# A decoder block's last layer: row columns taken from transposed tiles, products in three float32r terms, the expert choice moved behind a shift

## The chip, the core and the metric

The kernel runs on one core of a Trainium2 chip. TensorE does matrix products and transposes into PSUM, VectorE and ScalarE work on SBUF and PSUM, GpSimd on SBUF alone; SyncE and the others issue DMAs. The metric is the device time of one execution in microseconds; the median of several runs counts.

## The reference

Two transformer layers on x of 2 batches x 1024 rows x 256 columns. Each layer is a cross attention over 64 context rows with 16 heads, and a feed-forward part. The change touches only the second layer's end:

```python
def _layernorm(x, axis=-1, eps=1e-05):
    m = jnp.mean(x, axis=axis, keepdims=True)
    v = jnp.var(x, axis=axis, keepdims=True)
    return (x - m) / jnp.sqrt(v + eps)
...
    def _L1_ffn_ref(x, Wr, A, Bw):
        ...
        def _gates(cls_tok, Wr):
            logits = cls_tok @ Wr.T
            top_vals, top_idx = jax.lax.top_k(logits, K)
            neg_inf = jnp.full_like(logits, -jnp.inf)
            rows = jnp.arange(logits.shape[0])[:, None]
            masked = neg_inf.at[rows, top_idx].set(top_vals)
            return jax.nn.softmax(masked, axis=-1)
        gates = _gates(x[:, 0, :], Wr)
        mid = jnp.einsum('blh,erh->belr', x, A)
        expert_out = jnp.einsum('belr,ehr->belh', mid, Bw)
        weighted = jnp.einsum('be,belh->blh', gates, expert_out)
        return x + weighted
...
    x = x + _L1_xattn_ref(_layernorm(x, axis=-1), ctx_1024, ctx_1024, L1_xattn_Wq, L1_xattn_bq, L1_xattn_Wk, L1_xattn_bk, L1_xattn_Wv, L1_xattn_bv, L1_xattn_Wo, L1_xattn_bo)
    x = x + _L1_ffn_ref(_layernorm(x, axis=-1), L1_ffn_Wr, L1_ffn_A, L1_ffn_Bw)
```

The experts of a batch are chosen by its first row alone (K = 2 of E = 8, R = 64). So for each batch the kernel makes one 256x256 matrix, the weighed sum of the two experts' products, and multiplies every normalised row by it.

## The kernel before

The rows lie in 16 tiles of 128; two tiles make a unit, so there are NU = 8 units, even ones of batch 0, odd ones of batch 1. Each engine has one hand-written program, and semaphores tie them; what stands first in an engine's program runs first, and a wait holds all behind it.

The second attention runs unit by unit. Within step u, TensorE does scores(u,0), transposes of unit u-1's second half, the transposes of the next unit, project_o(u-2), values(u-1), scores(u,1), the query projection of the next unit (project_q), and the transposes of unit u's first half. VectorE does shift(u,0) and shift(u,1) (maximum, L507, and subtraction, L510) and between them the weighing of unit u-1 (weigh: L516, L519, L522, which makes oT). ScalarE does exponentials, copies out of PSUM and the logarithm in front of the weighing (L453, L455). GpSimd adds biases (L606) and subtracts the projected rows from x (residual, L613), and makes the reciprocal deviations of the norms (L115, L117).

The last layer's work is threaded into this loop by four tables (tensor_work, scalar_work, vector_work, gpsimd_work). Key 2u is a slot inside step u ahead of its second half, 2u+1 is its end, 16 lies behind the loop, "end" behind project_o(7). The steps of unit u of this last layer are: stats3 (VectorE), rstd3 (GpSimd), normalise3 (ScalarE), turn3 (four transposes on TensorE into one PSUM bank), copy3 (ScalarE), product3 (TensorE), add_norm (GpSimd adds the norm to x), add3 (VectorE adds the product), store (SyncE).

The choice of experts goes beside it: row_stats, row_rstd and row_norm normalise the two first rows alone, on one partition (L1617 to L1632); row_columns turns them into columns with eight tiny products (L1641); spread_columns copies each column to 128 (L1649); row_logits multiplies by the router weights (L1658); choose finds the two best experts (L1665 to L1675) with top_two; gates computes the weights; pick_factors gathers the two factors with indirect DMAs (L1702); weigh_second_factor scales one of them; batch_matrix makes the matrix (L1717) and keep_matrix copies it. product3 is in float32.

## Time and profile before

| what | value |
|---|---|
| time, median of 3 runs | 493.1 us (491.43 to 493.35) |
| the profiled execution's own time | 497.36 us |
| its span, from first to last instruction | 495.5 us |
| mean granted TensorE clock | 0.992 |
| busy: TensorE, VectorE, ScalarE, GpSimd | 95%, 58%, 40%, 48% of the span |

The times in the rows count from the span's start. A float32 product is two records of TensorE. The second attention begins at about 376 us; the last products end at 492.2 us, and the last store lands by 495.5 us.

### The profile page before, as it was taken

The page shows a single profiled execution, that of the slowest core. Times are in us where ns is not written, and L with a number is a line of the kernel's source. Part 1 is how long each engine was busy: PE and PEld are TensorE (multiplying, and loading weights), DVE is VectorE, ACT ScalarE, POOL GpSimd, SP SyncE. Part 2 cuts the span into 40 slices and gives each one's busy share as a digit, 9 for nine tenths or more (in the row PEclk, how much of TensorE's full clock was granted, in tenths as well). Part 3 has the DMA queues.
Part 4 walks back from the last instruction along what each step waited for, and adds up shares of the span by engine and source line. Part 5 has one row for each costly group of instructions (what it writes and reads, how often), then busy time and mean ns, then how long its engine had stood idle before and what let it go on. Part 6 is the DMA issues. An engine that isn't in the chain of part 4 may idle for free.

```text
span 495.5 us, 9491 instructions
## 1 busy us (share of the span) xinstructions
PE 468.4 (95%) x3132; PEld 385.0 (78%) x3132; DVE 286.6 (58%) x657; ACT 199.5 (40%) x447; POOL 236.0 (48%) x315
## 2 busy tenths in 40 slices
PE   7899999998999997998999999999997999899797
PEld 6677776686777786677999999999977676677576
DVE  5779985643461122325454545545457689998862
ACT  3455775557610021002323333232332456665641
POOL 6313344144337574219985543233232665753462
PEclk9999999999999999998999999999999899999999
DMA  8999300020003122999413332223117300000114
GB/s 280 392 404 351 41 12 1 1 85 2 0 1 111 69 103 84 340 309 331 70 48 102 108 87 70 82 65 86 34 42 238 104 2 1 1 3 0 31 34 150
DMA packets 48031, 52.98 MB, mean 107 GB/s; under 512 B 15313, under 2 KB 42258, under 8 KB 47730
## 3 DMA queue, kind: packets, MB, share of 16 engines
q1 hardware_dynamic: 34578, 23.02, 16.8%
q0 software_dynamic: 7616, 20.19, 12.3%
q10 hardware_dynamic: 5792, 9.18, 6.2%
q8 instruction: 28, 0.46, 0.4%
q14 instruction: 17, 0.14, 0.1%
HBM read 35.25 MB, written 17.12 MB: 106 GB/s over the span
## 4 chain that ended last, share of the span: by engine, by line
PE 75%; DVE 12%; ACT 4%; DMA 3%; issue 2%; another core or an unknown queue 1%; POOL 1%; ACTq 1%; SPq 0%; POOLq 0%; DVEq 0%
PE banks L1285 9%; PE banks L1232 9%; PE banks L1336 6%; PE banks L346 5%; PE banks L360 5%; PE banks L1337 5%; PE banks L1340 5%; PE banks L324 5%; PE banks L313 3%; PE banks L1358 3%; PE banks L1766 3%; PE banks L1362 3%; PE banks L1359 3%; PE banks L1348 3%; DVE mx L507 2%
## 5 line engine op out<-in xcount | busy, mean ns | idle before, releaser
L115 POOL TENSOR_TENSOR rstd<-var,mhalf 128x2 f32<-128x2 f32 x30 | 20.9, 696 | 86.1 <-DVE var L108 86.1
L1336 PE MATMUL banks<-w_hi,xgT_hi 128*128 x156 | 55.5, 356 | 2.8 <-ACT xgT_hi L966 2.3
L1162 ACT ACTIVATE hg<-banks 128x352 f32<-128x352 f32 x39 | 18.2, 466 | 98.6 <-PE banks L1340 89.0
L1509 DVE TENSOR_TENSOR hgT_lo<-banks,hgT_hi 128x256 fp32r<-128x256 f32 x78 | 24.1, 350 | 58.1 <-ACT hgT_hi L1169 56.7
L507 DVE TENSOR_REDUCE mx<-banks 128x16 f32<-128x1024 f32 x32 | 39.1, 1220 | 23.9 <-PE banks L324 23.7
L1337 PE MATMUL banks<-wd,xgT_hi 128*128 x156 | 51.0, 328 | 0.0
L1285 PE MATMUL banks<-sdn,big 128*128 128x256 f32 x192 | 47.5, 393 | 0.0
L1285 PEld LDWEIGHTS banks<-sdn,big 128*128 128x128 f32 x192 | 34.1, 189 | 12.6 <-issue 9.0
L1063 POOL DMA_INDIRECT expert_rows_in<-xn,slot x32 | 31.4, 982 | 20.7 <-issue 7.7
L324 PE MATMUL banks<-kvb,qT 64*128 64x256 f32 x256 | 36.7, 406 | 3.3 <-DVE ps L510 2.1
L1340 PE MATMUL banks<-w_hi,xgT_lo 128*128 x156 | 37.9, 325 | 0.0
L125 ACT ACTIVATE xn<-x,shift,rstd 128x256 f32<-128x256 f32 x60 | 32.9, 604 | 9.7 <-POOL shift L117 9.5
L1131 ACT ACTIVATE pw<-banks 128x512 f32<-128x512 f32 (+1 forms) x24 | 14.2, 593 | 53.0 <-issue 29.0
L1232 PE MATMUL banks<-xn2T_hi,sgu_hi 128*128 128x512 f32 x80 | 31.9, 399 | 2.9 <-DVE big L1475 2.9
L1336 PEld LDWEIGHTS banks<-w_hi,xgT_hi 128*128 128x128 f32 x156 | 29.9, 192 | 5.0 <-issue 4.5
L324 PEld LDWEIGHTS banks<-kvb,qT 64*128 64x128 f32 x256 | 22.5, 187 | 13.0 <-issue 9.1
L1094 POOL DMA_INDIRECT choices_out<-yy,dest x18 | 18.1, 1003 | 28.5 <-DVE yy L1502 21.1
L1232 PE MATMUL banks<-xn2T_lo,sgu_hi 128*128 128x512 f32 x80 | 31.2, 391 | 0.0
L1232 PE MATMUL banks<-xn2T_hi,sgu_lo 128*128 128x512 f32 x80 | 31.2, 390 | 0.0
L1358 PE MATMUL banks<-wd,hgT_hi 128*128 (+1 forms) x117 | 29.8, 284 | 0.7 <-ACT hgT_hi L1169 0.7
L1337 PEld LDWEIGHTS banks<-wd,xgT_hi 128*128 128x128 f32 x156 | 30.0, 192 | 0.2
L1359 PE MATMUL banks<-wd,hgT_hi 128*128 (+1 forms) x117 | 29.8, 283 | 0.0
(249 smaller groups left out, 1137.0 us busy)
## 6 DMA issues: line engine op xcount, KB each, us to landing
w_hi<-in_egu POOLq DMA_DIRECT2D x2, 2816.0 KB, 21.3
expert_rows_in<-zeros SPq DMA_DIRECT2D x1, 5304.0 KB, 40.3
xn<-expert_rows_in SPq DMA_DIRECT2D x39, 128.0 KB
y_all<-choices_out SPq DMA_DIRECT2D x16, 256.0 KB, 4.9
wd<-in_egu ACTq DMA_DIRECT2D x8, 352.0 KB, 9.7
wd<-in_egu ACTq DMA_DIRECT2D x4, 704.0 KB, 13.8
out_x<-x SPq DMA_DIRECT2D x8, 256.0 KB, 2.1
x<-in_x SPq DMA_DIRECT2D x2, 768.0 KB, 7.6
```

Of the source, the lines that this page charges most:

```text
L125: nc.scalar.activation(out[:, t, :], x[:, first + t, :], ACT.Identity, bias=m["shift"][:, b, t:t + 1], scale=m["rstd"][:, b, t:t + 1]).the ...
L324: last = nc.tensor.matmul(psS[:, r * 512 + hf * 256:r * 512 + hf * 256 + 256], qT[rows, u % 2, hf, t * P:(t + 1) * P], kb[batch_of(u)][row ...
L346: last = nc.tensor.matmul(psO[32 * j:32 * j + 32, k, w, :], lhs, pT[u % 2][:, 4 * k + j, :], start=True, stop=True, tile_position=(0, 32 * j))
L507: nc.vector.tensor_reduce(mx, heads(psS), AX.X, ALU.max).then_inc(max_done.sem, 1)
L1063: pool.indirect_dma_start(xg_dram[:, :], bass.IndirectOffsetOnAxis(ap=slot[:, j, t:t + 1], axis=0), xn2w[:, t, :], None, bounds_check=SLOT ...
L1232: last = nc.tensor.matmul(psum[bank][:, :], m[:, k, w * 6 * P + j * P:w * 6 * P + (j + 1) * P], v[g][:, k, :], start=(a == 0), stop=(a == ...
L1285: last = nc.tensor.matmul(psum[4 + c][:, t * D:(t + 1) * D], hT[0:SR[j], (g + 1) % 2, j, (2 * c + t) * P:(2 * c + t + 1) * P], sdn[0:SR[j] ...
L1336: nc.tensor.matmul(to, xgT_hi[:, c, k, :], hi, start=(k == 0), stop=False)
L1337: nc.tensor.matmul(to, xgT_hi[:, c, k, :], lo, start=False, stop=False)
L1340: last = nc.tensor.matmul(to, xgT_lo[:, c, k, :], w_hi[:, k, ds(e * (2 * I) + w * I, I)], start=False, stop=(k == KD - 1))
L1358: nc.tensor.matmul(psum[6][:, 0:D], h, d(k, 0), start=(k == 0), stop=False)
L1359: nc.tensor.matmul(psum[6][:, 0:D], h, d(k, 1), start=False, stop=False)
```

## The change

The two first rows are no longer normalised apart: the first column of the transposed tiles of units 0 and 1 is the row in question, so spread_columns copies from there (kept, an SBUF copy of the transposed tiles of units 0 to 3), and does it on GpSimd. row_stats, row_rstd, row_norm and row_columns are gone. product3 is split: each operand becomes a high part in float32r and the rest, and three products (high by high, high by low, low by high) take the place of one in float32. High parts of units 0 to 3 are made by ScalarE from kept (high_part), their rests by GpSimd (low_part); for units 4 to 7 the copy out of PSUM is the high part, and VectorE takes the rest (split3); VectorE also splits the matrices (split_matrix). The copy of the logits (take_logits) is split from choose, which moves one slot on. Unit 2 is multiplied before unit 1, the last unit has a PSUM bank for each tile and is added and stored tile by tile.

```diff
         def spread_columns():
-            nc.vector.wait_ge(f_rowT, 1)
-            for b in range(B):
-                for k in range(KD):
-                    v.tensor_copy(xcol[:, b, k, :], PSW[:, b * KD + k:b * KD + k + 1].to_broadcast([P, P])).then_inc(f_col, 1)
...
+            nc.gpsimd.wait_ge(f_xT, B)
...
+                    nc.gpsimd.tensor_copy(xcol[:, b, k, :], kept[:, b, k, 0:1].to_broadcast([P, P])).then_inc(f_col, 1)
...
+        def take_logits():
+            nc.vector.wait_ge(f_lg, 1)
+            v.tensor_copy(gt["p"][:, :, :], PSW[:, 64:64 + B * E].rearrange("p (b e) -> p b e", b=B)).then_inc(f_g, 1)
+
         def choose():
             nonlocal links
-            nc.vector.wait_ge(f_lg, 1)
-            v.tensor_copy(gt["p"][:, :, :], PSW[:, 64:64 + B * E].rearrange("p (b e) -> p b e", b=B)).then_inc(f_g, 1)
             nc.vector.wait_ge(f_g, 1)
...
+        def split_matrix(b):
+            nc.vector.wait_ge(f_wb, b + 1)
+            v.tensor_tensor(wb_lo[:, b, :, :], MATRIX_IN[b].rearrange("p (k n) -> p k n", k=KD),
+                            wb_hi[:, b, :, :].bitcast(F32), ALU.subtract).then_inc(f_wL, 1)
...
         def add_norm(u):
 
             wait(nc.gpsimd, ln3.xn_ready, UT * u + UT)
-            nc.gpsimd.wait_ge(f_row, 1 + B)
...
+            wait(nc.tensor, f_xL, u - KEPT)
...
+            to = kept[:, u, :, :] if u < KEPT else xT3_hi[:, u, :, :]
+            nc.scalar.activation(to, PSX.rearrange("p (k n) -> p k n", k=KD), ACT.Copy).then_inc(f_xT, 1)
+
+        def high_part(u):
+
+            nc.scalar.wait_ge(f_xT, u + 1)
+            nc.scalar.activation(xT3_hi[:, u, :, :], kept[:, u, :, :], ACT.Copy).then_inc(f_hi, 1)
+
+        def low_part(u):
+
+            nc.gpsimd.wait_ge(f_hi, u + 1)
+            nc.gpsimd.tensor_tensor(xT3_lo[:, u, :, :], kept[:, u, :, :], xT3_hi[:, u, :, :].bitcast(F32),
+                                    ALU.subtract).then_inc(f_lo, 1)
+
+        def split3(u):
+
+            nc.vector.wait_ge(f_xT, u + 1)
+            v.tensor_tensor(xT3_lo[:, u, :, :], PSX.rearrange("p (k n) -> p k n", k=KD), xT3_hi[:, u, :, :].bitcast(F32),
+                            ALU.subtract).then_inc(f_xL, 1)
 
         def product3(u):
-            nc.tensor.wait_ge(f_xT, u + 1)
-            nc.tensor.wait_ge(f_wb, min(u + 1, B))
+            nc.tensor.wait_ge(f_wL, u % 2 + 1)
+            if u < KEPT:
+                nc.tensor.wait_ge(f_lo, u + 1)
+            else:
+                nc.tensor.wait_ge(f_xL, u - KEPT + 1)
+                nc.tensor.wait_ge(f_added, ORDER.index(u - 4) + 1)
             if u < 2:
                 wait(nc.tensor, events1["exp_done"], 4 * NU)
-            wait(nc.tensor, f_added, u - 3)
+            terms = [(x, w, k) for k in range(KD) for x, w in ((xT3_hi, wb_hi), (xT3_hi, wb_lo), (xT3_lo, wb_hi))]
             for t in range(UT):
-                for k in range(KD):
-                    last = nc.tensor.matmul(MADE_IN[u][:, t * D:(t + 1) * D], xT3[:, u, k, t * P:(t + 1) * P],
-                                            wb[:, u % 2, k, :], start=(k == 0), stop=(k == KD - 1))
-            last.then_inc(f_y, 1)
+                to = LAST_IN[t][:, 0:D] if u == NU - 1 else MADE_IN[u][:, t * D:(t + 1) * D]
+                for m, (x, w, k) in enumerate(terms):
+                    last = nc.tensor.matmul(to, x[:, u, k, t * P:(t + 1) * P], w[:, u % 2, k, :],
+                                            start=(m == 0), stop=(m == len(terms) - 1))
...
+        def add_last():
+
+            nc.vector.wait_ge(f_summed, NU)
+            for t in range(UT):
+                nc.vector.wait_ge(f_y, NU + t)
+                row = unit_rows(NU - 1)[:, t, :]
+                v.tensor_tensor(row, LAST_IN[t][:, 0:D], row, ALU.add).then_inc(f_added, 1)
...
-        gpsimd_work = {7: lambda: (rstd3(0), first_rows()), 8: row_rstd, 9: lambda: rstd3(1), 11: lambda: (rstd3(2), add_norm(0)),
...
+        gpsimd_work = {7: lambda: (rstd3(0), first_rows()), 9: lambda: rstd3(1),
```

On VectorE, in step 7, the copy of the logits and the start of the choice (gc_ and gt_ are its small tiles) followed the weighing of unit 5 directly; shift(7,0) (mx and ps) came behind all of the choice:

```order
L519 SCALAR_TENSOR_TENSOR ninv<-err,inv 128x512
L522 TENSOR_TENSOR oT<-banks,ninv 128x512
L1665 COPY gt_p<-banks 128x16
L656 TENSOR_REDUCE gc_top<-gt_p 128x2
L657 TENSOR_TENSOR gt_key<-gt_p,gc_top 128x16
```

Now at the same place:

```order
L522 TENSOR_TENSOR oT<-banks,ninv 128x512
L1635 COPY gt_p<-banks 128x16
L507 TENSOR_REDUCE mx<-banks 128x16
L510 TENSOR_TENSOR ps<-banks,mx 128x1024
L656 TENSOR_REDUCE gc_top<-gt_p 128x2
```

The shift of unit 7's first half now stands ahead of the choice, and the choice between the two shifts. Further up on VectorE, stats3(4) has moved from behind the choice to ahead of shift(6,1).

GpSimd's program from step 5 to the gathers, before (L613 is the residual, L115 and L117 the deviations, L1741 add_norm):

```order
L613 TENSOR_TENSOR x<-x,o_rows 128x512
L115 TENSOR_TENSOR rstd<-var,mhalf 128x2
L117 TENSOR_TENSOR shift<-nmean,rstd 128x2
L1741 TENSOR_TENSOR x<-x,xn 128x512
L606 TENSOR_TENSOR x<-x,bo_all 128x256 x2
L613 TENSOR_TENSOR x<-x,o_rows 128x512
```

and now:

```order
L613 TENSOR_TENSOR x<-x,o_rows 128x512
L115 TENSOR_TENSOR rstd<-var,mhalf 128x2
L117 TENSOR_TENSOR shift<-nmean,rstd 128x2
L1620 COPY xcol<-kept 128x128 x4
L1718 TENSOR_TENSOR x<-x,xn 128x512
L1745 TENSOR_TENSOR xT_lo<-kept,xT_hi 128x512
L606 TENSOR_TENSOR x<-x,bo_all 128x256 x2
L613 TENSOR_TENSOR x<-x,o_rows 128x512
```

Four copies and a subtraction stand ahead of residual(4), the last row. Further on, rstd3(4) moves ahead of the residual in front of the gathers, and the gathers follow that residual at once; three more subtractions come in around them.

On TensorE around project_o(7) (L360), before (L1717 is batch_matrix, L1766 product3, L1750 turn3, L346 values(7)):

```order
L346 MATMUL banks<-pT_1,head_ones 32x256 x4
L1717 MATMUL banks<-fbg,fa 128x256 x4
L1766 MATMUL banks<-wb,xT 128x256 x4
L360 MATMUL banks<-wo,oT 128x256 x4
L1750 MATMUL banks<-ident,xn 128x128 x4
L1766 MATMUL banks<-wb,xT 128x256 x8
```

and the start of what stands there now:

```order
L1690 MATMUL banks<-fbg,fa 128x256 x2
L346 MATMUL banks<-pT_1,kvb 32x256 x4
L346 MATMUL banks<-pT_1,head_ones 32x256 x4
L346 MATMUL banks<-pT_1,kvb 32x256 x4
L346 MATMUL banks<-pT_1,head_ones 32x256 x4
L1690 MATMUL banks<-fbg,fa 128x256 x2
L1767 MATMUL banks<-wb_hi,xT_hi 128x256
L1767 MATMUL banks<-wb_lo,xT_hi 128x256
L1767 MATMUL banks<-wb_hi,xT_lo 128x256
```

Half of batch_matrix moved ahead of values(7). The three rows of L1767 repeat: two units of twelve, with turn3(5) between them, now stand ahead of project_o(7), and six units and two transposes behind it. On ScalarE, normalise3(5) and keep_matrix(0) now stand ahead of the last logarithm.

## Rows read from the trace of the kernel before

**Rows 1.** The page: clock in tenths over 40 slices; shares of the chain by engine.

```profile
PEclk9999999999999999998999999999999899999999
PE 75%; DVE 12%; ACT 4%; DMA 3%; issue 2%; another core or an unknown queue 1%; POOL 1%; ACTq 1%; SPq 0%; POOLq 0%; DVEq 0%
```

**Rows 2.** Chain of waits in order of time: start us, us, engine, tile, line, count.

```profile
427.24 1.16 DVE gc_nmean L1620
428.58 0.67 DVE stats L101 x2
...
438.54 0.98 PE banks L1641 x8
...
446.02 0.89 DVE xcol L1649 x4
```

**Rows 3.** Timeline, TensorE's idle times in brackets: start us, us, engine, line, tiles.

```profile
432.35 1.13 PE L324 MATMUL banks<-kvb,qT 64*128 64x256 f32 x8 [1.20 <-DVE ps L510]
...
447.04 1.97 PE L360 MATMUL banks<-wo,oT 128*128 128x256 f32 x8 [0.41 <-DVE xcol L1649]
```

**Rows 4.** The chain of waits further on.

```profile
460.43 1.23 DVE mx L507
...
464.22 1.24 DVE mx L507
...
468.81 1.99 PE banks L360 x8
...
492.20 0.69 DVE x L1775
```

**Rows 5.** Timeline: two GpSimd instructions and what VectorE did beside each.

```profile
409.92 1.29 POOL L613 TENSOR_TENSOR x<-x,o_rows 128x512 f32<-128x512 f32 x1
409.95 1.80 DVE L519 SCALAR_TENSOR_TENSOR ninv<-err,inv 128x512 f32<-128x512 f32 x1
...
467.31 1.02 POOL L1702 DMA_INDIRECT fb<-in_bw,picked  x1 [0.30 <-issue]
467.33 0.70 DVE L519 SCALAR_TENSOR_TENSOR ninv<-err,inv 128x512 f32<-128x512 f32 x1
```

**Rows 6.** Timeline: the choice's first and last instruction, residual, first gather, its use.

```profile
457.62 0.17 DVE L656 TENSOR_REDUCE gc_top<-gt_p 128x2 f32<-128x16 f32 x1
...
460.35 0.17 DVE L1675 CAST picked<-gc_row 128x2 int32<-128x2 f32 x1
...
460.98 1.28 POOL L613 TENSOR_TENSOR x<-x,o_rows 128x512 f32<-128x512 f32 x1 [7.55 <-ACT o_rows L460]
...
465.86 1.15 POOL L1702 DMA_INDIRECT fa<-in_a,picked  x1 [0.62 <-issue]
...
470.47 0.51 ACT L1710 ACTIVATE fbg<-fb,gcol 128x256 f32<-128x256 f32 x1 [1.94 <-DMA fb<-in_bw,picked]
```

**Rows 7.** Groups by line and shape: busy us, mean ns of one, idle before.

```profile
L204 POOL COPY ctx<-ctxT 128x128 f32<-128x128 f32 x4 | 1.4, 389 | 0.0
...
L1017 POOL TENSOR_TENSOR xn2T_lo<-turned,xn2T_hi 128x512 fp32r<-128x512 f32 x2 | 2.5, 1268 | 0.0
...
L1105 ACT ACTIVATE xn2T_hi<-turned 128x512 fp32r<-128x512 f32 x2 | 1.3, 634 | 0.1
```

**Rows 8.** Timeline of TensorE in the experts' down projection (float32r, 256 columns moving).

```profile
301.80 0.28 PE L1358 MATMUL banks<-wd,hgT_hi 128*128 x1
301.92 0.28 PE L1359 MATMUL banks<-wd,hgT_hi 128*128 x1
```

**Rows 9.** Timeline of the end: last logarithm, project_o(7), then transposes and float32 products.

```profile
473.25 0.58 ACT L453 ACTIVATE inv<-banks 128x512 f32<-128x512 f32 x1
...
476.87 1.89 PE L360 MATMUL banks<-wo,oT 128*128 128x256 f32 x8
...
478.60 0.60 PE L1750 MATMUL banks<-ident,xn 128*128 128x128 f32 x4
...
479.04 3.62 PE L1766 MATMUL banks<-wb,xT 128*128 128x256 f32 x16
...
482.49 0.60 PE L1750 MATMUL banks<-ident,xn 128*128 128x128 f32 x4
```

More of the change, by code:

```diff
@@ L1601, in xattn_ffn_kernel @@
         MADE_IN = [psum[(u + 2) % 4] for u in range(NU)]
+        LAST_IN = [psum[(NU + 1) % 4], psum[5]]
+        ORDER = [0, 2, 1, *range(3, NU)]
         def link(ins):
@@ L1804, in load_ffn1 @@
             sp.dma_start(wr[:, :, :], split(wr_in)).then_inc(ffn1_in, 16)
-        tensor_work = {"keys and values": lambda: keep_warm(nc, psum[0], mem["ident"], 26), 9: lambda: turn3(0), 10: row_columns, 11: lambda: turn3(1), 12: row_logits,
-                       13: lambda: turn3(2), 15: lambda: turn3(3), "last output but one": lambda: turn3(4),
-                       16: lambda: (batch_matrix(0), batch_matrix(1), product3(0)),
-                       "end": lambda: (turn3(5), product3(1), product3(2), turn3(6), product3(3), product3(4),
-                                       turn3(7), product3(5), product3(6), product3(7)),
-                       "x6": lambda: nc.tensor.wait_ge(f_xT, 1), "x7": lambda: nc.tensor.wait_ge(f_xT, 2),
-                       "o4": lambda: nc.tensor.wait_ge(f_col, B * KD), "o5": lambda: nc.tensor.wait_ge(f_g, 1)}
@@ L1820, in xattn_ffn_kernel @@
-        vector_work = {6: lambda: stats3(0), 8: lambda: (row_stats(), stats3(1)), 9: lambda: (row_norm(), second_half_rows()), 10: lambda: stats3(2),
-                       11: spread_columns, 12: lambda: stats3(3), 13: choose, 14: lambda: stats3(4), 15: gates,
-                       "last output but one": lambda: stats3(5), 16: lambda: stats3(6),
-                       "end": lambda: (stats3(7), *(add3(u) for u in range(NU)))}
-        gpsimd_work = {7: lambda: (rstd3(0), first_rows()), 8: row_rstd, 9: lambda: rstd3(1), 11: lambda: (rstd3(2), add_norm(0)),
-                       13: lambda: (rstd3(3), add_norm(1)), 15: lambda: (rstd3(4), pick_factors(0), pick_factors(1), add_norm(2)),
-                       16: lambda: (rstd3(5), add_norm(3), rstd3(6), add_norm(4), rstd3(7),
-                                    add_norm(5), add_norm(6), add_norm(7))}
+        tensor_work = {"keys and values": lambda: keep_warm(nc, psum[0], mem["ident"], 26), 9: lambda: turn3(0), 11: lambda: turn3(1), 12: row_logits,
+                       13: lambda: turn3(2), 14: lambda: turn3(3), 15: lambda: turn3(4),
+                       "last output but one": lambda: batch_matrix(0),
+                       16: lambda: (batch_matrix(1), product3(0), turn3(5), product3(2)),
+                       "end": lambda: (turn3(6), product3(1), product3(3), product3(4), turn3(7), product3(5), product3(6),
+                                       product3(7)),
+                       "x6": lambda: nc.tensor.wait_ge(f_xT, 1), "x7": lambda: nc.tensor.wait_ge(f_xT, 2),
+                       "o5": lambda: nc.tensor.wait_ge(f_g, 1)}
@@ new lines, in xattn_ffn_kernel @@
+        vector_work = {6: lambda: stats3(0), 8: lambda: stats3(1), 9: second_half_rows,
+                       10: lambda: stats3(2), 12: lambda: (stats3(3), stats3(4)), 13: take_logits, 14: choose,
+                       15: lambda: (gates(), split3(4), stats3(5)), "last output but one": lambda: (stats3(6), split_matrix(0)),
+                       16: lambda: (split_matrix(1), split3(5), add3(0)),
+                       "end": lambda: (stats3(7), add3(2), add3(1), split3(6), add3(3), add3(4), split3(7), add3(5), add3(6),
+                                       add_last())}
@@ new lines, in xattn_ffn_kernel @@
+        gpsimd_work = {7: lambda: (rstd3(0), first_rows()), 9: lambda: rstd3(1),
+                       11: lambda: (rstd3(2), spread_columns(), add_norm(0), low_part(0)),
+                       13: lambda: (rstd3(3), rstd3(4), add_norm(1), low_part(1), low_part(2)),
+                       15: lambda: (pick_factors(0), pick_factors(1), rstd3(5), add_norm(2)),
+                       16: lambda: (low_part(3), rstd3(6), *(add_norm(u) for u in range(3, 6)), rstd3(7), add_norm(6), add_norm(7))}
```

71 lines of the change are left out of this document (26 added, 45 removed).

## The prediction

> **What bounds the kernel now.** I read the page first, then the chain of waits in order of time, then the timeline of the last 70 us. The page says that TensorE carries 75% of the chain and VectorE 12%, and that TensorE is granted its full clock nearly throughout, the tenths near 1.0 being its 2.4 GHz level [rows 1]. The edits all lie after 425 us of a 495.5 us span, so only that stretch needs pricing. The reader is to see two regimes in it. Up to about 472 us the chain changes hands between VectorE and TensorE: the lone-row statistics stand on it at 427.24, the products that turn the row into a column at 438.54, the spreading at 446.02 [rows 2], and the first score shift of the last unit starts at 460.43, directly behind the expert choice [rows 4, 6]. From 476.87 on it is TensorE alone, with project_o(7), transposes and products to the last add at 492.20 [rows 4, 9]. The two need different working: in the first a removed step gives only what the next late engine leaves; in the second every matmul saved counts whole.
>
> All times below are on the clock of the profiled execution, and are worked as a lead over it. That execution took 497.36 us (span 495.5), the median of the runs is 493.1. I take the gain off the median; a ratio of 0.991 between the two changes a few us by nothing.
>
> **The change in its tail, TensorE alone.** A product in float32 of 128x256 is two records; two units of four products each and one transpose group run from 478.60 to 482.49, of which the transposes take 0.44 (478.60 to 479.04), so a unit costs (3.89 - 0.44)/2 = 1.73 us [rows 9]. The changed unit has 12 float32r products. The nearest row is the expert down projection: float32r, 128x128 weights reloaded for each, 256 columns moving, 0.12 us from one to the next [rows 8]. 12 x 0.1175 = 1.41 us. From the start of project_o(7), before: 1.73 for itself, 3 x 0.44 of transposes, 7 units x 1.73 = 15.2 us. After: only 6 units and 2 transpose groups remain, since product 2 and turn3(5) now stand ahead of project_o(7): 1.75 + 0.9 + 8.5 = 11.1 us. Gain **4.1**, if no wait opens. The one near to opening is turn3(7): residual, statistics, rstd and normalisation of unit 7 take some 4.6 us behind project_o(7), and TensorE has 0.44 + 3 x 1.41 = 4.7 us of work there; I count nothing and keep 0.5 for the range. The last add in halves of 128x256, each stored at once, takes about half of the 0.69 us [rows 4] off the end: gain **0.3**.
>
> **The row's columns.** Leaving out the row statistics on VectorE (427.24 is one of six instructions) lets statistics and shift of unit 4 start that much sooner; what TensorE gets is its own idle time there, 1.2 us before 432.35 [rows 2, 3]. The eight records at 438.54 go: 0.98 us [rows 2]. Against it, ScalarE makes a high part of each kept tile, 0.63 us in the like operation [rows 7], ahead of the normalisation of unit 6, which TensorE's transposes now reach early: loss 0.4. TensorE's wait for the spreading before project_o(4) was 0.41 [rows 3]: gain. Lead by then 2.2 us. Spreading moves to GpSimd: four copies of 128x128 at 0.39 [rows 7] = 1.6 us, followed in the same queue by add_norm(0), low_part(0), the bias add and residual(4), four instructions at about 1.3 us (1.27 for the like subtraction, [rows 7]). GpSimd can start at about 442.9 (the second transposed tile), so residual(4) ends near 449.8. stats3(4) is moved ahead of VectorE's shift (6,1) and waits for exactly that residual; with 1.24 us of its own (428.58 to the next instruction) it ends at 451.1, where the shift's scores are ready at 450.8. Behind it queue the shift and all of TensorE's unit 7. Loss 0.3: lead **1.9 us**. Bounds: copies between nearly 0 and 0.7 each put it at 2.2 and 0.9.
>
> **The choice.** Before, VectorE chose for 2.9 us (457.62 to 460.5, some 14 small instructions [rows 6]) and only then shifted the first half of unit 7. Now only the copy out of PSUM stays ahead and the choice follows that shift. Its place is then between the two shifts, 456.1 + 2.5 = 458.6 to 461.5, where the scores for the second shift are ready at 461.3 anyway: that alone would bring the second shift from 464.22 to 461.5, a lead of 2.7. But now there is GpSimd work beside it. Where a GpSimd add ran beside VectorE's scalar_tensor_tensor with two SBUF operands, it took 1.80 us (409.95, the add at 409.92); beside a gather issue it took 0.70 (467.33) [rows 5]. It looks held until GpSimd's instruction ends. So residual(5), due at 459.4, holds the choice for 0 to 1.2 us. I take it whole: second shift at 462.6, lead **1.6 us**, and 1.4 at project_o(6) (467.4 against 468.81 [rows 4]). The Trainium skill, GPSIMD Engine Reference, section 8 (Key points), states the cause: GpSimd shares its SBUF interfaces with VectorE and contends with VectorE instructions that have two SBUF inputs. By that rule the sum below stands; without it, it would be rival A's.
>
> **The gathers.** They start right behind the choice, no longer behind rstd3(4): at 462.8 against 465.86. The first pair was used 4.6 us after the first issue (470.47 [rows 6]), so it lands at 467.4, before gates() has the weights at 468.0. Thus the gathers' latency, 1.94 us of ScalarE idling, leaves the path. batch_matrix(0) (0.87) now stands before values(7), in place of a transpose (0.44): lead 1.0 at its end.
>
> **The last weighing.** Before, the logarithm started at 473.25 and project_o(7) at 476.87 [rows 9]. Now ScalarE's queue has normalise3(5), which waits for rstd3(5), and keep_matrix(0) ahead of it: 0.5 us lost. VectorE's two-operand step of that weighing now meets add_norm(3) on GpSimd, which is busy without a pause there: up to 1.3, I take 1.0. So project_o(7) starts at about 477.3: lead **-0.4**. If the step isn't held, TensorE still has product 0, turn3(5) and product 2 to do until 476.8, and the lead is about 0.
>
> **Sum.** -0.4 + 4.1 + 0.3 = 4.0 us, 493.1 - 4.0 = **489.1 us**. A measurement of this kernel can tell about 0.5% (2.5 us) from no change.
>
> **Rivals.**
> A, the holds don't bite. If the residual doesn't hold the choice, all behind it comes 1.1 us sooner, and project_o(7) leads by +0.7, or by +1.1 if the weighing isn't held either: gain 5.1 to 5.5, 487.6 to 488.0 us. For it: VectorE's instructions of the choice are short and may get in first.
> B, GpSimd becomes the bound. It takes eight instructions more (four copies, four subtractions, 1.6 + 5.1 us), in a queue through which residual, rstd and gathers pass. Each us that it is late before stats3(4) or rstd3(7) comes off whole; with 1 to 2.5 us lost, the gain is 1.5 to 3: 490.1 to 491.6 us. For it: the 0.3 us by which stats3(4) is late already. Against: GpSimd idled 7.55 us before the residual at 460.98, between units [rows 6].
> C, slower: the pace of the three-term products. It is one mechanism: if a float32r product with changing weights goes at the float32 record's 0.217 us (3.45/16 [rows 9]), not 0.12, a unit costs 2.6 us. Then project_o(7) starts at 479.2 (2.3 late), 6 units behind it cost 15.6 in place of 12.1 with 7, and the end comes 5.0 later: 498.1 us. It decides from 0.165 us a product (24 of them ahead of project_o(7), 72 behind). The down projection's rows speak against it; for it, only that its operands come from other tiles.
> D, it doesn't do what it says: the chain hangs on something untouched. Then about 493. Against it: the tail's products are the chain [rows 4, 9].
>
> **How the numbers follow.** Forecast (3.2 to 5 us gained) 0.50; A 0.22; B 0.19; C 0.04; D 0.05. Over 2.5 us faster: 0.50 + 0.22 + half of B and a little = 0.83; same 0.12; slower 0.05. The range, 486.8 to 491.4, takes A with 0.8 us for the runs' own spread and most of B, and leaves out C and D.
>
> **What would show it.** Right: 12 products of a unit in about 1.41 us; scores (5,0) without idle time; the second shift of unit 7 at 461.5 to 462.6; the first gather right behind the picked rows; 11 to 11.5 us from project_o(7) to the end of the products. Wrong: a product spacing over 0.13; TensorE idle before turn3(7); VectorE idle before stats3(4) for residual(4) by more than 0.5 us; the choice taking over 4.2 us.

## The result and the profile after

The changed kernel takes **486.95 us** (median of 4 runs, 486.51 to 488.73) beside 493.23 us before (4 runs, 491.43 to 494.80): the ratio is 0.9877, with a 95% interval of 0.9842 to 0.9912, so 4.3 to 7.8 us are gained. 489.1 us was forecast. The profiled execution took 488.73 us, with a span of 487.0; before, 497.36 and 495.5.

| us | before | after |
|---|---|---|
| median time | 493.23 | 486.95 |
| span of the profiled execution | 495.5 | 487.0 |
| start of scores(4,1) | 426.44 | 422.87 |
| from there to the end of the span | 69.06 | 64.13 |

The two spans differ by 8.5 us, more than the times, and the last two rows say why. The first place at which both programs do the same work right ahead of the edits is TensorE's scores for the second half of unit 4. It comes 3.57 us sooner after the change, though no edit stands in TensorE's way up to there. The chain of waits of before shows where this is from; its rows are start, duration and what was running:

```profile
178.40 3.11 PE banks L1232 x12
...
181.59 0.69 DVE big L1475
182.28 6.31 another core or an unknown queue
...
189.51 5.73 PE banks L1232 x24
...
196.60 3.41 PE banks L1285 x14
```

The third row is VectorE's wait for something that the profile does not name; TensorE stood idle for 2.95 us of it. The same products in the chain of the changed kernel:

```profile
178.27 13.60 PE banks L1232 x60
...
193.23 6.83 PE banks L1285 x28
```

So something arrived late in that execution of before. The first products of L1285 start at 196.60 there and at 193.23 here, 3.37 us apart. So 3.4 of the 3.6 us belong to one execution. The traces of this study reach scores(4,1) between 420.3 and 426.4 us, though up to there the kernels differ only in a few small instructions (the clamps named below and the first row's statistics). All comparisons of traces below therefore count from scores(4,1). What the edits give by that clock is 69.06 - 64.13 = **4.93 us**, within the interval of the times.

The page of the changed kernel, the chain's shares by engine:

```profile
PE 77%; DVE 7%; ACT 6%; DMA 4%; issue 3%; POOL 1%; ACTq 1%; SPq 0%; POOLq 0%
```

TensorE carries a little more of the chain than before and VectorE less [rows 1]. The chain from the choice to the last add, the counterpart of [rows 2] and [rows 4]:

```profile
456.02 1.24 DVE gt_key L657
458.59 0.59 issue
459.42 0.39 POOL fa L1675
...
463.52 2.94 DMA fb<-in_bw,picked
466.54 0.37 ACT fbg L1683
466.96 1.08 ACT xn L125 x2
468.03 0.49 ACT wb_hi L1696
468.54 0.70 DVE wb_lo L1701
469.29 1.69 PE banks L1767 x12
470.98 0.44 PE banks L1728 x4
471.42 1.43 PE banks L1767 x12
472.85 1.96 PE banks L360 x8
474.81 0.44 PE banks L1728 x4
475.24 4.32 PE banks L1767 x36
479.56 0.44 PE banks L1728 x4
480.00 4.32 PE banks L1767 x36
484.34 0.42 DVE x L1785
```

The last six rows are the tail: from project_o(7) at 472.85 there is no waiting row up to the last add. 36 products of L1767 take 4.32 us, that is 0.12 each and 1.44 for a unit, where a unit had cost 1.73 [rows 9]. Above them stands what the forecast had not put on the path: the landing of the second unit's factors (2.94), and behind it a row of small steps on ScalarE and VectorE that ends at the first product.

VectorE's choice, in its timeline (start, duration, line, operation), and GpSimd's residual beside it:

```profile
454.58 0.16 DVE L656 TENSOR_REDUCE gc_top<-gt_p 128x2 f32<-128x16 f32 x1
454.77 0.17 DVE L657 TENSOR_TENSOR gt_key<-gt_p,gc_top 128x16 f32<-128x16 f32 x1
...
456.02 1.23 DVE L657 TENSOR_TENSOR gt_key<-gt_rest,gc_top 128x16 f32<-128x16 f32 x1
...
458.36 0.17 DVE L1648 CAST picked<-gc_row 128x2 int32<-128x2 f32 x1
458.45 1.22 DVE L507 TENSOR_REDUCE mx<-banks 128x16 f32<-128x1024 f32 x1
```

```profile
455.94 1.27 POOL L613 TENSOR_TENSOR x<-x,o_rows 128x512 f32<-128x512 f32 x1 [2.12 <-ACT o_rows L460]
459.42 1.16 POOL L1675 DMA_INDIRECT fa<-in_a,picked  x1 [2.20 <-DVE picked L1648]
```

The operation of L657 takes 0.17 us at 454.77 and 1.23 at 456.02, beside the residual, and ends 0.04 us after it. This is the hold of [rows 5] again, now on a tile of 128x16. The whole choice takes 3.95 us (454.58 to 458.53), 2.90 before. The first gather starts 0.9 us behind the picked rows.

The stages, each counted in us from the start of scores(4,1), where "shift" is VectorE's maximum (L507) of a half unit, and the leads of after over before next to those that were forecast:

| | shift(6,1) | shift(7,1) | project_o(6) | project_o(7) | end of last add | end |
|---|---|---|---|---|---|---|
| before | 26.53 | 37.78 | 42.37 | 50.43 | 66.45 | 69.06 |
| after | 24.71 | 35.58 | 40.16 | 49.94 | 61.89 | 64.13 |
| lead | 1.82 | 2.20 | 2.21 | 0.49 | 4.56 | 4.93 |
| forecast | 1.9 | 1.6 | 1.4 | -0.4 | | 4.0 |

### The profile page after: what moved, and what is told of

Its sections match the earlier page's. It is cut to its first block, busy times and chain, and to the rows that moved or that the text cites. A ratio compares the mean times of both kernels' runs of the same rounds, so it can differ in the third digit from the quotient of the medians.

```text
span 487.0 us, 9539 instructions
## 1 busy us (share of the span) xinstructions
PE 465.0 (95%) x3156; PEld 383.3 (79%) x3156; DVE 289.7 (59%) x652; ACT 201.2 (41%) x451; POOL 240.8 (49%) x321
## 4 chain that ended last, share of the span: by engine, by line
PE 77%; DVE 7%; ACT 6%; DMA 4%; issue 3%; POOL 1%; ACTq 1%; SPq 0%; POOLq 0%
PE banks L1232 10%; PE banks L1285 10%; PE banks L1336 6%; PE banks L346 5%; PE banks L1337 5%; PE banks L360 5%; PE banks L1340 5%; PE banks L324 5%; PE banks L313 5%; PE banks L1358 3%; PE banks L1362 3%; PE banks L1359 3%; PE banks L1348 3%; PE banks L1767 2%; ACT xn L125 2%
## 5 line engine op out<-in xcount | busy, mean ns | idle before, releaser
L115 POOL TENSOR_TENSOR rstd<-var,mhalf 128x2 f32<-128x2 f32 x30 | 20.8, 695 | 82.6 <-DVE var L108 82.6
L507 DVE TENSOR_REDUCE mx<-banks 128x16 f32<-128x1024 f32 x32 | 39.1, 1221 | 22.5 <-PE banks L324 22.4
L1285 PE MATMUL banks<-sdn,big 128*128 128x256 f32 x192 | 47.5, 393 | 0.0
L1285 PEld LDWEIGHTS banks<-sdn,big 128*128 128x128 f32 x192 | 34.1, 189 | 12.6 <-issue 9.0
```

Of the source, the lines that this page charges most:

```text
L507: nc.vector.tensor_reduce(mx, heads(psS), AX.X, ALU.max).then_inc(max_done.sem, 1)
L1285: last = nc.tensor.matmul(psum[4 + c][:, t * D:(t + 1) * D], hT[0:SR[j], (g + 1) % 2, j, (2 * c + t) * P:(2 * c + t + 1) * P], sdn[0:SR[j] ...
```

## The experiments

Each kernel is the changed one with the edit shown, unless it says before. In all of them the expert numbers that TensorE's registers load are clamped to zero from below, which lets line numbers rise by 3 or 4. Nothing of what is computed is left out in any. Numbers are from the profiled execution, counted from scores(4,1), unless a ratio to the kernel before is given.

**The yardstick.** The changed kernel with only the clamp.

> The changed kernel itself, with one addition that all my kernels carry: the expert numbers that TensorE's program loads are clamped at zero in a second register before they are waited against (40 small register operations, all before the second attention). It is the yardstick for the others. Both theories expect 0.5 us or less beside the changed kernel, so 5 to 7 us under the kernel before, and in its profile the same stretch from the second attention's first product to the last add as in the changed kernel's (some 108.5 us).

487.32 us (6 runs, 486.75 to 489.15), ratio 0.9898 [0.9868, 0.9929]. The stages repeat those of the table within 0.02 us (end 64.13). Two executions of one kernel agree that closely behind scores(4,1), so a few tenths of a us can be read from one trace, as long as the clock stays up (below).

The medians tell less. The same work was timed three times in this study, as the changed kernel, as this yardstick and once more at the end: 486.95, 487.32 and 489.16 us. A part of that is TensorE's clock. In eight of the fourteen traces it falls to 1.2 GHz for 3.4 us, once or more, in code that no edit touches (at about 120, 224 or 385 us): twice in the traces of before and after, never in the yardstick's. A run's mean granted clock tells how much of that it had. The yardstick's three runs at 1.000 took 486.75 to 487.55 us, the two at 0.993 took 488.77 and 489.15. So what an edit gives is read from the traces below, and medians are compared only for a first check.

**The products' pace.** Back to float32 with one term; the tiles are float32 too, and the order and the splitting work are kept.

```
-            ... for k in range(KD) for x, w in ((xT3_hi, wb_hi), (xT3_hi, wb_lo), (xT3_lo, wb_hi))]
+            ... for k in range(KD) for x, w in ((xT3_hi, wb_hi),)]
```

> Undoes the pace alone: the products of a unit are four in float32 again, the tiles are float32, and all splitting work is still done (it computes zeros), so order, waits and the other engines' work are those of the changed kernel. Theory A (behind project_o(7) only TensorE's work counts, and a unit costs 1.41 us in place of 1.73): 6 units behind it cost 6 x 0.32 = 1.9 us more, and the two ahead of it 0.0 to 0.6, as their cover by the last weighing allows: 1.9 to 2.6 us slower than the yardstick. Rival B (the gain came from the steps that left VectorE upstream; the pace is hidden): within 0.7 us of it.

491.24 us, ratio 0.9965 [0.9945, 0.9984]; the end comes at 66.16, 2.03 us later. Its tail in the chain:

```profile
474.63 5.18 PE banks L1770 x24
479.81 0.44 PE banks L1731 x4
480.25 5.20 PE banks L1770 x24
```

5.18 us for three units against 4.32: 0.29 us a unit is what the three terms save. Six units behind project_o(7) and two ahead of it make 2.3, and 2.03 arrive, within what was expected. The medians are 3.9 us apart; the runs of both kernels with a mean clock of 0.993 are 2.4 apart (491.3 and 489.0). By the traces the change of the products alone is worth about two fifths of the whole gain.

**The choice's hold.** residual(5) on GpSimd moved from ahead of the gathers to behind them (late_residual is the function residual).

```
-            if 2 <= u < by_pool + 2:
+            if 2 <= u < by_pool + 2 and not (bo is not None and u == NU - 1):
                 residual(u - 2)
...
-                        15: lambda: (pick_factors(0), pick_factors(1), rstd3(5), add_norm(2)),
+                        15: lambda: (pick_factors(0), pick_factors(1), mem["late_residual"](NU - 3), rstd3(5), add_norm(2)),
```

> Moves one GpSimd instruction, residual(5), from ahead of the gathers to behind them, so that it no longer runs beside the expert choice on VectorE. Theory A (two-operand VectorE instructions are held while a GpSimd add runs): the choice takes 2.9 to 3.0 us and not 3.95, the second shift of unit 7, project_o(6) and the first gather come 1.0 us sooner. The end gains 0 to 0.8 us, since ScalarE's queue (second gather, normalise3(5), keep_matrix(0)) and the last weighing's own hold are next. Rival C (the choice is long for another reason, such as its own chain of waits): the choice keeps its 3.95 us, nothing moves but statistics 5, which come later by up to 0.4 us.

The choice shrinks from 3.95 to 2.89 us and the first gather comes 1.06 us sooner, so the hold was real. shift(7,1) stays at 35.58 to the hundredth. VectorE now idles there for TensorE:

```profile
457.55 1.23 DVE L507 TENSOR_REDUCE mx<-banks 128x16 f32<-128x1024 f32 x1 [0.97 <-PE banks L324]
```

So the hold ran beside scores that were not ready before the choice ended, and cost the path nothing. The end moved against what was expected, to 65.73, 1.60 later (489.98 us, ratio 0.9943 [0.9919, 0.9967]), because the residual found another victim, the first instruction of the gates:

```profile
462.00 1.92 DVE L1661 TENSOR_SCALAR gc_den<-gc_e 128x2 f32<-128x2 f32 x1
```

```profile
461.57 1.01 POOL L1679 DMA_INDIRECT fb<-in_bw,picked  x1 [0.30 <-issue]
462.61 1.28 POOL L613 TENSOR_TENSOR x<-x,o_rows 128x512 f32<-128x512 f32 x1
```

An instruction on 128x2 numbers took 1.92 us, and ended as the residual did. In the changed kernel it takes 0.29. Behind it wait both gates, the weighted factors and batch_matrix(0): the instruction is 1.63 us longer, and project_o(7) comes 1.61 us later.

**The choice ahead of the first shift again**, in the changed kernel.

```
-                        13: take_logits, 14: choose,
+                        13: lambda: (take_logits(), choose()),
```

> The changed kernel with the choice put back ahead of unit 7's first shift, directly behind the copy of the logits. After the last result (without the hold, the second shift came no sooner, since its scores were ready only then) theory A says: the first shift comes 2.9 us later, the second shift 0 to 1.3 us later than in the changed kernel, the gathers 2.5 to 3.5 us sooner, and the end between 0.7 us sooner and 1.3 us later. Rival E: the place of the choice is worth 2 us or more at the end.

492.03 us, ratio 0.9973 [0.9949, 0.9997]; shift(7,1) comes 2.52 us later, the end 2.36 later, which is the rival's case and not the theory's. The choice takes 5.02 us there, since GpSimd has two instructions beside it that hold it:

```profile
452.00 1.20 DVE L658 TENSOR_TENSOR gt_key<-gt_key,rev 128x16 f32<-128x16 f32 x1
...
455.34 1.26 DVE L1651 CAST picked<-gc_row 128x2 int32<-128x2 f32 x1
```

The two holds make 2.1 of the 5.02 us; no run has the choice at that place without them. Inside the changed kernel the place of the choice is worth 2.4 us at the end, more than any other single edit.

**The two upstream parts alone, on the kernel before.** First the columns: they come from the transposed tiles, and the row's statistics, deviation, normalisation and eight products are gone.

```
-            nc.vector.wait_ge(f_rowT, 1)
+            nc.vector.wait_ge(f_xT, B)
...
-                    v.tensor_copy(xcol[:, b, k, :], PSW[:, b * KD + k:b * KD + k + 1].to_broadcast([P, P])).then_inc(f_col, 1)
+                    v.tensor_copy(xcol[:, b, k, :], xT3[:, b, k, 0:1].to_broadcast([P, P])).then_inc(f_col, 1)
```

> The kernel before with one part of the change alone: the columns of the two first rows are copied from the transposed tiles (on VectorE, in the slot where the spreading stood), and the lone-row statistics, the eight tiny products and their waits are gone. Products stay in float32, the choice stays whole and in its place. Theory A (these steps lay on the path up to the last weighing, and before it nothing else was near): measured from the shift of unit 4's second half, the first shift of unit 7, project_o(6) and project_o(7) come 1.8 to 2.4 us sooner than in the kernel before, and so does the end. Rival D (the gathers or the choice absorb it): project_o(7) comes less than 1 us sooner.

490.84 us, ratio 0.9944 [0.9919, 0.9969]. shift(6,1) is at 23.63, a lead of 2.90; the end is at 66.23, a lead of 2.83, where 1.8 to 2.4 was expected. From scores(4,1) to 456.78 us TensorE's timeline shows no wait. Then the choice alone: take_logits ahead of the first shift, choose behind it, and the exponential of the gates (gate_exp, on ScalarE) one slot later.

```
-                        13: choose, 14: lambda: stats3(4)
+                        13: take_logits, 14: lambda: (choose(), stats3(4))
```

> The kernel before with another part alone: the copy of the logits is split from the choice, which goes behind the first shift of unit 7, with the exponential of the gates one slot later on ScalarE. Statistics 4 stay behind the choice. Theory A: the same work stands between the two points on VectorE, so the first shift comes 2.9 us sooner, but the second, and with it the gathers, comes no sooner, and 0 to 1.3 us later, by what the residual on GpSimd holds the choice; the end 0.5 us sooner to 1.5 us later. Rival E (moving the choice is by itself what brings the gathers and unit 7 forward): the second shift 1 us or more sooner, and the end too.

496.64 us, ratio 1.0052 [1.0027, 1.0076]: slower, outside what was expected. shift(7,1) comes 0.87 us later than before, since the choice (held for 1.3 us at L662) and stats3(4) now both stand ahead of it. That is only a quarter of the 3.46 us lost at the end. The rest is the clock. TensorE's timeline, then busy times in windows (the number behind POOL's is the granted clock, a share of 2.4 GHz):

```profile
463.26 1.46 PE L335 MATMUL banks<-ident,ps 128*128 128x128 f32 x8 [2.96 <-DVE ps L510]
465.31 3.78 PE L360 MATMUL banks<-wo,oT 128*128 128x256 f32 x8 [0.59 <-DVE oT L522]
```

```profile
463.00:464.00 1.00, 0.74 (x6) 0.75 (x7) 0.97 (x3) 0.11 (x2) 0.70 (x1) 0.92 0.00 0
464.00:465.00 1.00, 0.71 (x4) 0.31 (x2) 0.97 (x2) 0.80 (x2) 0.99 (x1) 0.50 0.41 139
```

After the idle 2.96 us the clock went to 0.50, its level of 1.2 GHz, and stayed there to 470.7, 6.8 us in all. project_o(6) took 3.78 us for the same eight products that take 1.99 at the full clock. Between it and project_o(7) the lag grows from 0.86 to 3.39 us, while TensorE has no idle time: 10.59 us for what took 8.06 before. The median of 12 runs is 3.0 us above that of the kernel before beside it, and none of the 12 has a mean clock over 0.995, so this trace is no exception. So the choice between the shifts does not pay by itself. In the changed kernel, where stats3(4) is out of its way, it does; that stats3(4) makes the difference is argued from the order on VectorE and was not tested alone.

**The hold of the last weighing.** GpSimd's adds wait until the last oT is written.

```
-                        16: lambda: (low_part(3), rstd3(6), *(add_norm(u) ...
+                        16: lambda: (low_part(3), rstd3(6), wait(nc.gpsimd, events1["oT_ready"], NU), *(add_norm(u) ...
```

> Makes GpSimd wait for the last weighing before add_norm(3), so that nothing of it runs beside the weighing's scalar_tensor_tensor. Theory A: that instruction takes 0.70 us and not 1.62, oT comes 0.9 us sooner, at which point products 0 and 2 are next, ending 0.05 us before it came: project_o(7) gains 0.1 us at most, and the end 0 to 0.2 us; GpSimd's three adds come 2 us later, and nobody waits for them. Rival: GpSimd's adds are then late for rstd3(7), TensorE waits before the last transposes, 0.5 to 1 us slower.

In the changed kernel VectorE's step took 1.62 us instead of 0.69. It started during the first of three adds in a row on GpSimd:

```profile
470.42 1.62 DVE L519 SCALAR_TENSOR_TENSOR ninv<-err,inv 128x512 f32<-128x512 f32 x1
```

```profile
470.21 4.21 POOL L1718 TENSOR_TENSOR x<-x,xn 128x512 f32<-128x512 f32 x3
```

Here it takes 0.69 again, 0.93 us less. project_o(7) comes 0.17 us sooner and the end 0.28, a little more than expected. The products 0 and 2 cover the rest of the hold. The median, 488.61 us (ratio 0.9917 [0.9887, 0.9947]), is 1.3 us above the yardstick's all the same: four of its 12 runs have a mean clock of 0.99 (490.33 to 492.76 us), and its three at 1.000 took 485.88 to 487.25, on average 0.4 us less than the yardstick's three.

**What the changed kernel lacks beside the columns alone.** There shift(6,1) was at 23.63, here at 24.71. Two suspects: ScalarE's rounding copies, and GpSimd's spreading. First, high_part(0) and high_part(1) put into ScalarE's idle time:

```
-                        "exps4": lambda: (copy3(0), high_part(0)), 10: ...
-                        "exps5": lambda: (copy3(1), high_part(1)), 12: ...
+                        "exps4": lambda: copy3(0), "inverse5": lambda: high_part(0), 10: ...
+                        "exps5": lambda: copy3(1), "inverse6": lambda: high_part(1), 12: ...
```

> The changed kernel with the rounding copies of the first two units (high_part(0) and high_part(1), 0.63 us each on ScalarE) moved from ahead of a normalisation into ScalarE's idle time behind inverse(4) and inverse(5); everything else as in the changed kernel. Beside the added columns alone the changed kernel is 1.08 us late at the second shift of unit 6 (24.71 against 23.63 us after scores(4,1)). Theory: most of that is TensorE's two waits for ScalarE's normalised rows before the transposes of L291 (0.30 and 0.34 us in the changed kernel). Then both waits go, scores(5,1) starts 0.3 us and the second shift of unit 6 some 0.5 to 0.65 us sooner (24.05 to 24.2), and the end moves by less, 0.1 to 0.6 us sooner, since the choice, which is still held by residual(5), ends where it did relative to its own start. Rival: TensorE waits at the next place for VectorE instead (its shifts run one behind the other), the second shift of unit 6 stays within 0.15 us of 24.71, and what the changed kernel lacks beside the columns alone is the work added on GpSimd.

Second, the spreading on VectorE in place of GpSimd, in its slot 11:

```
-                    nc.gpsimd.tensor_copy(xcol[:, b, k, :], kept[:, b, k, 0:1].to_broadcast([P, P])).then_inc(f_col, 1)
+                    nc.vector.tensor_copy(xcol[:, b, k, :], kept[:, b, k, 0:1].to_broadcast([P, P])).then_inc(f_col, 1)
```

> The changed kernel with the four copies that spread the routed rows' columns moved from GpSimd to VectorE, in its slot 11 (ahead of stats3(3)), where the columns-alone kernel has them too. Theory: GpSimd's 1.00 us for them costs nothing at the end, because stats3(4), which they delay through residual(4), was done 0.6 us before its shift; so the second shift of unit 6 stays at 24.7 us after scores(4,1) and the end within 0.3 us of the changed kernel's. The wait of stats3(4) for residual(4) (1.24 us) gets shorter by up to 1 us. Rival: GpSimd's chain of adds is what separates the changed kernel from the columns alone; then the second shift of unit 6 comes 0.4 to 1.0 us sooner.

The first brings shift(6,1) to 23.63, the very place of the columns alone and 0.4 us sooner than expected; the second leaves it at 24.73 and the end at 64.11, as expected (one run, 488.53 us). So all of the 1.08 us is ScalarE's. These are the waits in the timeline of the changed kernel (TensorE, transposes of the next unit); both are gone when the copies are moved:

```profile
429.96 0.66 PE L291 MATMUL banks<-ident,xn 128*128 128x128 f32 x4 [0.30 <-ACT xn L125]
...
441.24 0.66 PE L291 MATMUL banks<-ident,xn 128*128 128x128 f32 x4 [0.34 <-ACT xn L125]
```

They show 0.30 and 0.34 us idle but cost 0.52 and 0.56. Without the wait the transposes' row even starts before the row ahead of it has ended: in the run with the copies moved at 426.89, the other ending at 427.05. With the copies moved, shift(7,1) leads by another 1.09 and project_o(6) too (39.07), yet project_o(7) only by 0.25 and the end by 0.39 (63.74). One run, 485.77 us. What took the rest stands in the next paragraphs.

**All of it together.** residual(5) behind the gates and not only behind the gathers; the last adds behind the last weighing; the products 0 and 2 both ahead of turn3(5), and ScalarE's and VectorE's steps there in the order in which TensorE needs them.

```
-                        16: lambda: (batch_matrix(1), product3(0), turn3(5), product3(2)),
+                        16: lambda: (batch_matrix(1), product3(0), product3(2), turn3(5)),
...
-                        15: lambda: (pick_factors(0), pick_factors(1), rstd3(5), add_norm(2)),
+                        15: lambda: (pick_factors(0), pick_factors(1), nc.gpsimd.wait_ge(f_gcol, 2), mem["late_residual"](NU - 3), rstd3(5), add_norm(2)),
```

> A try at a better order on top of the changed kernel: residual(5) goes behind the gathers and waits for the gates (so that it holds neither the choice nor the gates, as it did the gates in the last run: 1.92 us for their first instruction); ScalarE makes the last logarithm before normalise3(5); matrix 0 is split before statistics 6; products 0 and 2 both stand ahead of turn3(5); GpSimd's adds wait for the last weighing; add3(0) stands behind the last residual. Theory A (what bounds project_o(7) is ScalarE's queue and the hold): project_o(7) 1.0 to 1.5 us sooner, and the end as much, 0.9 to 1.5 us under the yardstick. If statistics 5 or 7 come too late for the transposes, TensorE waits in the tail and the gain is 0 to 0.5 us.

project_o(7) is at 49.10 and the end at 63.31, 0.82 us sooner, a little under what was expected; 488.15 us, ratio 0.9884 [0.9854, 0.9914], which the times cannot tell from the yardstick's 0.9898. Then the same with the two rounding copies moved, and the changed kernel once more beside it:

> The combined order (residual(5) behind the gates, the last unit's weighing clear of GpSimd's adds, the products 0 and 2 ahead of turn3(5)) with high_part(0) and high_part(1) in ScalarE's idle time too. The combined order ended 0.82 us sooner after scores(4,1) than the changed kernel (63.31 against 64.13). Theory: the two waits of 0.30 and 0.34 us on TensorE go and, with the choice no longer held, all of that reaches the end: 62.7 to 63.0 us after scores(4,1), a time 1.1 to 1.5 us under the changed kernel's. Rival: the choice or the gathers are next, and the end is at 63.2 to 63.4.

> The changed kernel once more, unchanged in its work, as yardstick on the same chip for the combined order: 486.5 to 488.5 us, and 64.13 us from scores(4,1) to the end of the span.

487.01 us (ratio 0.9868 [0.9838, 0.9898]) for the combined order against 489.16 (0.9910 [0.9883, 0.9938]) for the changed kernel on the same chip: 2.15 us apart by the medians, with intervals that still overlap. The 489.16 is 0.7 us above what was expected, and the 2.15 is more than the 1.1 to 1.5 expected. Up to project_o(6) the combined order is 1.10 us ahead (39.07 against 40.17), as expected. The end is at 63.89, later than without the moved copies and outside what theory and rival had said, and the changed kernel itself ends at 64.90 this time instead of 64.13. Both traces have this in TensorE's timeline (here the changed kernel's):

```profile
460.92 1.09 PE L335 MATMUL banks<-ident,ps 128*128 128x128 f32 x8 [1.12 <-DVE ps L510]
462.97 3.67 PE L360 MATMUL banks<-wo,oT 128*128 128x256 f32 x8 [0.95 <-DVE oT L522]
```

```profile
462.00:463.00 1.00, 0.05 (x2) 0.03 (x1) 0.97 (x3) 0.70 (x2) 0.86 (x1) 1.00 0.40 123
463.00:464.00 1.00, 1.00 (x3) 0.82 (x4) 0.87 (x5) 0.26 (x1) 0.69 (x2) 0.50 0.20 41
```

and the yardstick, an execution of the same kernel with the same waits:

```profile
459.79 1.09 PE L335 MATMUL banks<-ident,ps 128*128 128x128 f32 x8 [1.12 <-DVE ps L510]
461.84 1.99 PE L360 MATMUL banks<-wo,oT 128*128 128x256 f32 x8 [0.96 <-DVE oT L522]
```

with the granted clock at 1.00 throughout. In three traces (this one, the moved copies alone and the combined order with them) the clock fell to 1.2 GHz for 3.4 us at project_o(6), behind waits of 1.12 and 0.95 us. In nine other traces with the same two waits it did not fall. For one kernel the fall cost 0.84 us at project_o(7) and 0.77 at the end. The run with the moved copies alone lacks the same 0.84: it is 1.09 ahead at project_o(6) and 0.25 at project_o(7). The combined order lacks twice that: 1.10 ahead of its version without the moved copies at project_o(6), 0.53 behind it at project_o(7), 1.63 us in all. There TensorE has no idle time between the two (8.93 us busy of 8.93), and 3.4 us at half the clock put off 1.7 us of its work, an estimate that fits. How the two kernels end with the clock up was not seen, so that the fall took all of it is not shown.

## Why the prediction was right, and where not

The forecast gain was 4.0 us; 4.93 are in the traces and 6.3 (4.3 to 7.8) in the times. The time lies inside the range. The 1.35 us by which the medians go beyond the 4.93 are less than the spread of either kernel's runs, and the rows of the two chains at 180 us show how much one late arrival moves a run.

- **The tail: right in its mechanism, and by luck to the tenth.** Forecast 4.1 and 0.3. From project_o(7) to the end of the last add 16.02 us became 11.95, and another 0.37 is gained behind it, since half of the last unit is already stored: 4.44 in all, against 4.4. Up to the start of the last add it is 3.80 (15.33 became 11.53), not 4.1, since project_o(7) took 1.96 instead of 1.75 and six units 8.64 instead of 8.5; the last add and the store give 0.64, not 0.3. 12 products take 1.44 us against 1.41, no wait opened before turn3(7).
- **The row's columns: right in size up to shift(6,1)** (1.82 against 1.9), by terms that were off both ways, so the size is luck. With the columns alone the lead is 2.90, more than the 2.6 of the sum's idle and record terms (1.2, 0.98 and 0.41). ScalarE's rounding copies were charged 0.4 once; there are two ahead of shift(6,1) and together they cost 1.08.
- **GpSimd's spreading: cover underrated.** Four copies took 1.00 us, not 1.6. stats3(4) did wait 1.24 us for the residual, which the forecast named as a sign of failure over 0.5:

```profile
445.70 0.75 DVE L101 BATCH_NORM_STATS2 stats<-x 128x6 f32<-128x256 f32 x2 [1.24 <-POOL x L613]
...
447.58 1.23 DVE L507 TENSOR_REDUCE mx<-banks 128x16 f32<-128x1024 f32 x1 [0.58 <-PE banks L324]
```

  The 0.58 in the second row is what was left over: the 0.3 of loss never came. The sign was badly chosen. It is the idle time before the shift that tells, not the one before the statistics.
- **The choice: mechanism right, charged to the wrong account.** This is the step that failed. The hold was forecast at up to 1.2 us and measured 1.06, beside the residual that was named. But the forecast put it whole on the path ("second shift at 462.6"). The scores of that half were ready only when the held choice ended: in the run with the hold removed the shift did not move. On the clock of before (3.57 us added) the held choice ended at 462.1 and the scores at 462.0, where the forecast had 462.6 and 461.3, so a hold priced at 1.1 us cost nothing there. The lead at shift(7,1) is 2.20 instead of 1.6, at project_o(6) 2.21 instead of 1.4. That is 0.8 of the 0.9 us by which the sum fell short. The result is near rival A's time, though not by its mechanism: the hold bites and has cover.
- **From project_o(6) to project_o(7): right in sum, by luck.** The lead falls by 1.72, against 1.8 forecast. The hold of the last weighing was 0.93 (forecast 1.0), but only 0.17 of it is on the path. In its place stands what the forecast had called gone, the gathers. This is read from the chain; no run moves the gathers by themselves. The first pair does not wait for data, but for the gates; the second pair does, and ScalarE's queue carries that wait to normalise3(5) and the matrix:

```profile
463.81 0.51 ACT L1683 ACTIVATE fbg<-fb,gcol 128x256 f32<-128x256 f32 x1 [1.04 <-DVE gcol L1660]
466.54 0.51 ACT L1683 ACTIVATE fbg<-fb,gcol 128x256 f32<-128x256 f32 x1 [2.23 <-DMA fb<-in_bw,picked]
```

- **The rivals.** B did not come: taking the four copies off GpSimd moved the end by 0.02 us, and holding its last adds back did not delay it. C is excluded by 0.12 us a product and by the float32 run.

The Trainium skill, SBUF — State Buffer, section "Who interferes with whom", says more than the forecast used: VectorE contends with GpSimd not only with two SBUF inputs but also in copies, casts and tensor_scalar in their two-port modes, and whoever comes first holds the ports for the whole instruction. The rows above agree: a CAST took 1.26 us and a TENSOR_SCALAR 1.92 where they had taken 0.17 and 0.29. The TENSOR_SCALAR started 0.6 us ahead of the residual, during a gather's issue, so something held it before the residual did; that it was the issue is likely, not shown. By the rule with two inputs alone, the gates of the run with the late residual would have passed unheld.

## What to carry to other kernels

Before a hold or a wait is charged to the path, look at what the instruction behind it waits for on its other side: the same 1.06 us hold cost nothing in one place, and 1.6 us when it was moved to where nothing covered it. Small instructions on tiny tiles suffer most from a neighbour's hold, measured by their own length (0.17 us became 1.23), and they stand in chains. GpSimd's large adds are better placed beside VectorE's work on PSUM: in the trace of before the shift at 429.73, whose two instructions read PSUM, took 1.21 and 1.23 us beside two GpSimd adds, and 1.22 and 1.22 at 435.11 with GpSimd idle. To compare single executions, count from the last common point ahead of the edits, and look at the granted clock around every wait of TensorE before a late stage is explained by the code.

## What the hardware showed that was not expected

- TensorE's clock fell to its 1.2 GHz level behind short waits: 2.96 us (choice alone), 2.45 us (choice first), and in three of twelve traces behind 1.12 and 0.95 us with 1.09 us of work between them. It lasted 3.4 to 6.8 us. Behind the 2.45 us it cost nothing that shows: the lag is 2.52 us ahead of it and at project_o(6). Where project_o(6) fell into it, it took 3.5 to 3.8 us instead of 1.99. The Trainium skill, TensorE: Matmul & The Clock Gate, Part 1, says that how many matmuls go at the low clock differs from run to run of the same kernel. The two executions above, 0.77 us apart, agree.
- VectorE's instruction on 128x2 numbers took 0.17 to 1.92 us, by what GpSimd did beside it. A gather's issue does it only at times. The first instruction of the gates took 0.29 and 0.28 us in the changed kernel and the yardstick, where it started 0.7 us into an issue of 1.01, and ended with it; started 0.04 us into one (before, and the columns alone) or 0.44 (the combined order) it took 0.16. The two-input step beside a gather had its usual 0.70 [rows 5]. The hold goes both ways: in the changed kernel GpSimd's add of 471.44, the second of the three, took 1.74 us instead of 1.27 beside that VectorE step.
- GpSimd copies one column of 128x128 spread over its tile in 0.25 us, while a plain 128x128 copy had taken 0.39 [rows 7].
